# One attention-and-FFN layer in one program: VectorE's first take ahead of the last row half, its inversion behind the second take, and GpSimd's sums beside the exponentials

## What is computed

```python
x = x + xattn(layernorm(x), ctx)       # x: 8 x 1024 x 512, ctx: 8 x 64 x 512, 16 heads of 64
x = x + ffn(layernorm(x))
# xattn: q = ln(x) Wq, k, v = ln(ctx) Wkv; softmax(clip(q k / 8, -11, 11)) v Wo + bo
# ffn:   h = silu(xq Wg) * (xq Wu); out = hq Wd, every operand rounded to 8-bit steps (fake quantization)
```

## Time and profile before

| | us |
|---|---|
| three runs of the kernel, median (lowest, highest) | 1312.22 (1311.52, 1313.82) |
| the profiled execution | 1311.13 |
| its span, first to last instruction | 1309.2 |
| TensorE busy in it | 1263.4 |
| VectorE busy | 1093.7 |
| ScalarE busy | 800.9 |
| GpSimd busy | 277.1 |

### The profile page before, as it was taken

The page is one execution under the profiler, slowest core; times in us unless marked ns, Lnnn a source line. Parts: engine busy times, 40 slices in busy tenths (PEclk is TensorE's granted clock), DMA queues, the critical chain, the costliest instruction groups (busy, mean ns, idle before and its releaser), DMA issues.

```text
span 1309.2 us, 20493 instructions
## 1 busy us (share of the span) xinstructions
PE 1263.4 (96%) x7607; PEld 583.7 (45%) x7607; DVE 1093.7 (84%) x2117; ACT 800.9 (61%) x1211; POOL 277.1 (21%) x227
## 2 busy tenths in 40 slices
PE   6999899999999999999999999999999999999998
PEld 4644444444444444444444443444444444434443
DVE  7777878878877877887787768799999999889998
ACT  6688576567558657756765772233333333399993
POOL 2105231441342144034224330000000000013233
PEclk9999899999999999999999999999999999999999
DMA  8276156248156264452553392196667542389997
GB/s 297 81 234 185 35 144 203 79 108 222 57 140 191 77 179 133 118 197 73 153 197 91 99 245 106 41 307 211 219 257 264 203 170 85 113 313 417 419 418 304
DMA packets 182436, 241.74 MB, mean 185 GB/s; under 512 B 122032, under 2 KB 141248, under 8 KB 169920
## 3 DMA queue, kind: packets, MB, share of 16 engines
q1 hardware_dynamic: 182336, 240.43, 55.8%
HBM read 120.86 MB, written 90.57 MB: 161 GB/s over the span
## 4 chain that ended last, share of the span: by engine, by line
PE 33%; DVE 27%; ACT 16%; POOL 9%; issue 8%; DMA 7%; SPq 1%; POOLq 0%; ACTq 0%; DVEq 0%
PE pg L1575 11%; PE pu L1581 11%; POOL esum L396 8%; ACT hb L1439 4%; ACT E L453 3%; DVE E L668 3%; DVE p L672 3%; ACT E L459 3%; DVE st L608 3%; ACT E L463 2%; PE po L77 2%; PE po L79 2%; PE po L78 2%; DVE st L682 2%; DVE x L679 2%
## 5 line engine op out<-in xcount | busy, mean ns | idle before, releaser
L1417 ACT ACTIVATE sg<-pg,gate_scale 128x512 f32<-128x512 f32 x176 | 120.9, 687 | 183.5 <-PE pg L1575 183.5
L77 PE MATMUL po<-VW,p 128*128 128x512 f16 x480 | 183.4, 382 | 14.0 <-DVE x_rows L679 10.4
L77 PE MATMUL ring<-yT,M 128*128 128x512 f16 x512 | 194.4, 380 | 0.0
L79 PE MATMUL ring<-yT,M 128*128 128x512 f16 x512 | 194.3, 380 | 0.0
L78 PE MATMUL ring<-yT,M 128*128 128x512 f16 x512 | 194.3, 380 | 0.0
L79 PE MATMUL po<-VW,p 128*128 128x512 f16 x480 | 183.2, 382 | 0.0
L78 PE MATMUL po<-VW,p 128*128 128x512 f16 x480 | 183.0, 381 | 0.0
L1575 PE MATMUL pg<-xqT,w 128*128 128x512 bf16 x704 | 180.7, 379 | 1.0 <-ACT xqT L1428 0.8
L1581 PE MATMUL pu<-xqT,w 128*128 128x512 bf16 x704 | 180.7, 380 | 0.0
L474 ACT ACTIVATE p<-E 128x512 f16<-128x512 f32 x120 | 74.7, 623 | 164.1 <-DVE E L668 164.0
L1491 DVE TENSOR_TENSOR hb<-pu,sg 128x512 f32<-128x512 f32 x176 | 120.8, 687 | 26.5 <-PE pu L1581 25.0
(11 more groups left out here) (238 smaller groups left out, 2017.9 us busy)
## 6 DMA issues: line engine op xcount, KB each, us to landing
hidden<-hb SPq DMA_DIRECT2D x11, 2816.0 KB, 9.7
xa<-x_rows_d SPq DMA_DIRECT2D x28, 1024.0 KB, 5.8
hb<-hidden SPq DMA_DIRECT2D x22, 1024.0 KB, 16.2
x<-in_x_dram SPq DMA_DIRECT2D x16, 1024.0 KB, 6.4
value_fold<-E SPq DMA_DIRECT2D x64, 256.0 KB, 2.5
VW<-value_fold SPq DMA_DIRECT2D x16, 1024.0 KB, 6.6
x_rows_d<-x SPq DMA_DIRECT2D x16, 1024.0 KB, 4.1
out_dram<-xa SPq DMA_DIRECT2D x11, 1024.0 KB, 12.9
```

The source lines that it names most:

```text
L77: nc.tensor.matmul(out, a_hi, b_hi, start=first, stop=False)
L79: return nc.tensor.matmul(out, a_lo, b_hi, start=False, stop=last)
L1417: nc.scalar.activation(sg[:, n % 4], pg[n % 4][:], ACT.Silu, scale=gate_scale[:, n % FT:n % FT + 1]).then_inc(silus, 1)
```

## The change

What it does, engine by engine:

- VectorE, steps 2 to 14: the fourth row half of group s+1 (`low_y(s+1, 3)`) moves from the score part behind take 0; `unit_range` moves from in front of take 0 behind folds 0 to 3; `invert` moves from in front of take 1 behind folds 4 to 7. `take` is split in `take_sum` and `take_stats`, which together are the same instructions.
- GpSimd: the adds of a group follow its exponentials in all steps; the four biases come behind the adds, and wait for `prob_lo` only. In step 0 they no longer lie between the adds.
- Steps 0 and 1: statistics and rsqrt of group 2 move from step 0 to step 1; its four rows are normalized and split at the end of step 1. The probabilities of group 0 are divided, made high and low with one tile beside each score tile, where they were bunched later.
- The end (behind the scores of group 15): the inversion comes in front of take 0, the splits of group 15 come earlier among the takes of group 14, the first two takes of group 15 surround `centre`, and `round_unit(14)` goes behind them.

```diff
--- before.py
+++ after.py
@@ -226,17 +226,15 @@
     def highs_beside(s, t):
 
         if s == 1:
-            return ((), (), (0,), (1,), (2, 3), (4,), (5,), (6, 7))[t]
+            return (t,)
         return (t + 2,) if s > 1 and t < 6 else ()
 
     def row_beside(s, t):
 
-        if s + 1 == NG:
-            return None
-        return {5: 2, 7: 3}.get(t) if s == 1 else {3: 0, 4: 1, 6: 2, 7: 3}.get(t)
+        return {3: 0, 4: 1, 6: 2, 7: 3}.get(t) if 1 < s and s + 1 < NG else None
 
     NORM_BESIDE = ((), (), (), (0, 1), (), (2,), (3,), ())
-    LOW_BESIDE = ((), (), (), (), (0,), (1,), (), (2, 3))
+    LOW_BESIDE = ((), (), (), (), (0,), (1,), (), (2,))
 
     FOLD_AFTER = ((0, 1, 2, 3), (4, 5, 6, 7), (), ())
 
@@ -406,14 +404,10 @@
 
         for s in range(NG):
             more = s + 1 < NG
-            if s > 1 and more:
-                pool.wait_ge(prob_lo, 8 * s)
-                pool.wait_ge(y_lo, 4 * (s + 1) + TT)
             for t in range(1, KT):
                 add_up(s, t)
-                if s == 0 and t >= 4:
-                    bias(s + 1, t - 4)
-            if s > 0 and more:
+            if more:
+                wait(pool, prob_lo, 8 * s)
                 for t in range(TT):
                     bias(s + 1, t)
 
@@ -573,9 +567,6 @@
                 if s > 0 and row_beside(s, t) is not None:
                     high_y(s + 1, row_beside(s, t))
                 exp(s, t)
-                if s == 1 and t == 1:
-                    high_y(2, 0)
-                    high_y(2, 1)
                 if s == 0:
                     if t in (0, 2):
                         wo_high(2 + t // 2)
@@ -586,6 +577,9 @@
                         fold_value(0, t)
             if s == 0:
                 continue
+            if s == 1:
+                for t in range(TT):
+                    high_y(2, t)
             for t in range(TT):
                 for u in FOLD_AFTER[t]:
                     fold(s, u)
@@ -671,13 +665,16 @@
             dve.wait_ge(prob_hi, 8 * g + t + 1)
             nc.vector.tensor_tensor(probs(g, 1, t), E[:, g % 2, t], probs(g, 0, t), ALU.subtract).then_inc(prob_lo, 1)
 
-        def take(g, t):
+        def take_sum(g, t):
             if t == 0:
                 dve.wait_ge(x_scaled, g + 1)
             dve.wait_ge(outs, 4 * g + t + 1)
             xt, row = x[:, g % 4, t], keep.rows[:, TT * g + t]
             nc.vector.tensor_tensor_reduce(xt, po[t % 2][:], xt, keep.out_scale[:], -3e38,
                                            ALU.add, ALU.max, row[:, 2:3]).then_inc(outs_taken, 1)
+
+        def take_stats(g, t):
+            xt, row = x[:, g % 4, t], keep.rows[:, TT * g + t]
             dve.wait_ge(outs_taken, 4 * g + t + 1)
             nc.vector.bn_stats(st1[:, t, :], xt).then_inc(x1_step, 1)
             nc.vector.tensor_reduce(row[:, 3:4], xt, AX.X, ALU.min)
@@ -685,6 +682,10 @@
             ins = nc.vector.bn_aggr(row[:, 0:2], st1[:, t, :])
             if t == TT - 1:
                 ins.then_inc(x1_seen, 1)
+
+        def take(g, t):
+            take_sum(g, t)
+            take_stats(g, t)
 
         def unit_range(u):
             dve.wait_ge(f_loaded, 16 * (2 * min(u + 1, FT) + max(u + 1 - FT, 0)))
@@ -928,18 +929,16 @@
                     if t % 2 == 1:
                         fold_value(0, t - 1)
                         fold_value(0, t)
-                    if t == 4:
-                        norm_stats(2)
+                    continue
+                if s == 1:
+                    if t in (2, 3):
+                        norm_stats(2, (2 * t - 4, 2 * t - 3))
                     if t == 5:
                         norm_aggregates(2)
-                    if t == 6:
                         norm_rstd(2, 2)
-                    continue
-                if s == 1:
-                    if t in (4, 6):
-                        norm_rows(s + 1, t // 2)
-                    if t in (5, 7):
-                        low_y(s + 1, t // 2)
+                    if t == 7:
+                        norm_rows(2, 0)
+                        norm_rows(2, 1)
                     continue
                 if not more:
                     continue
@@ -953,47 +952,58 @@
                 for k in NORM_BESIDE[t]:
                     norm_rows(s + 1, k)
             if s == 0:
-                norm_rows(2, 0)
-                norm_rows(2, 1)
                 invert(0)
-                low_y(2, 0)
-                low_y(2, 1)
                 continue
+            if not more:
+                continue
+            if s == 1:
+                for t in range(2):
+                    low_y(2, t)
+                    norm_rows(2, t + 2)
+                low_y(2, 2)
+            take(s - 1, 0)
+            low_y(s + 1, 3)
+            for u in FOLD_AFTER[0]:
+                fold(s, u)
             if s <= UNITS:
                 unit_range(s - 1)
-            take(s - 1, 0)
-            if more:
-                for u in FOLD_AFTER[0]:
-                    fold(s, u)
+            take(s - 1, 1)
+            for u in FOLD_AFTER[1]:
+                fold(s, u)
             invert(s)
-            if more:
-                take(s - 1, 1)
-                for u in FOLD_AFTER[1]:
-                    fold(s, u)
-                round_unit(s - 1)
-                take(s - 1, 2)
-                for u in FOLD_AFTER[2]:
-                    fold(s, u)
-                divide(s, 0)
-                take(s - 1, 3)
-                divide(s, 1)
-                low(s, 0)
+            round_unit(s - 1)
+            take(s - 1, 2)
+            for u in FOLD_AFTER[2]:
+                fold(s, u)
+            divide(s, 0)
+            take(s - 1, 3)
+            divide(s, 1)
+            low(s, 0)
         last = NG - 1
+        unit_range(last - 1)
+        invert(last)
+        take(last - 1, 0)
+        for t in range(3):
+            divide(last, t)
+        low(last, 0)
         take(last - 1, 1)
-        divide(last, 0)
-        divide(last, 1)
-        low(last, 0)
-        round_unit(last - 1)
-        take(last - 1, 2)
-        for t in range(2, KT):
+        low(last, 1)
+        for t in range(3, 5):
             divide(last, t)
             low(last, t - 1)
-            if t == 5:
-                take(last - 1, 3)
+        take_sum(last - 1, 2)
+        for t in range(5, KT):
+            divide(last, t)
+            low(last, t - 1)
         low(last, KT - 1)
+        take_stats(last - 1, 2)
+        take(last - 1, 3)
         keep.range_of_rows(dve, 0, TT * last)
+        take(last, 0)
         keep.centre(dve)
-        for t in range(TT):
+        take(last, 1)
+        round_unit(last - 1)
+        for t in range(2, TT):
             take(last, t)
 
     def on_tensor(pe):
```

## The result

| | before | after |
|---|---|---|
| median of the runs, us (lowest, highest) | 1312.95 (1311.52, 1313.82) | 1292.16 (1290.38, 1292.80) |
| ratio, 95% interval | | 0.9841 [0.9823, 0.9858] |
| the profiled execution, its span | 1311.13, 1309.2 | 1292.56, 1290.8 |

The account below looks back on a forecast made before the run. TensorE, busy 96% of the span, was taken as the bound, so only removing its waits pays. Steady steps -19.5, start +4.8, end -4.3 gave -19.0, written -19.1: 1293 us on the median's scale, range 1287 to 1306.

Parts of the forecast that it names:

- The 12.4 us for the bank: Steady steps: TensorE's twelve waits for VectorE's L679, the sum emptying a PSUM bank, were to go, gaining 12.4 us.
- The 7.1 us of folds: Steady steps: fifteen waits of TensorE's last fold products for VectorE's low halves were to go, gaining 7.1 us.
- The sums beside the exponentials: Steady steps: seven GpSimd adds of 1.27 us per step, each costing VectorE 0 to 1.27 us, were to stay hidden.
- 5 to 7 us a step: Expected sign in steady steps: VectorE's L672, L633 and rsqrt rows up to 1.27 us longer, 5 to 7 us a step.
- The eighth split: Score part: the eighth tile's split was to end at 3.2; TensorE wants it at 4.5, leaving 1.2 us to spare.
- the rivals: One more collision, two more, three or more, change does nothing: 1302.7, 1312.7, 1328, 1313 us; chances 0.13, 0.05, 0.09, 0.03.
- one more add: Rival: another add meets a two-SBUF instruction ahead of the eighth split; 9.6 us lost, 1302.7 us; chance 0.13.
- the cap: Steady steps: the last tile's cap, freeing the ring for the second fold, was to end at 5.8 against 5.9.
- Start: Steps 1 and 2: losses of 10.3 us against 6.2, and 0.7 in step 2: +4.8 us, bounds 0 to +8.
- The half clock: Step 1: a 5.8 us stall at the folds was to halve TensorE's clock again, costing 2.2 us.
- End: Last four outputs: 2.4 us of split waits and 1.9 at low clock were to go: -4.3 us, bounds -2 to -4.3.
- keeps for small waits: In the sum: 0.1 us of the -19.0 us total set aside for small waits, written as -19.1.

## Why the prediction held, point by point

- **The bound** was read rightly: TensorE's waits are the account, and three quarters of the last chain is now TensorE. The 12.4 us for the bank went with the inversion moved behind take 1.
- **The 7.1 us of folds went, but the step that explained them failed.** "Take 0 goes ahead of the last row half ... The 7.1 us go" gave them to that move. Alone it costs 25 us; the inversion alone removes them. I had worked out that VectorE enters the score part over 2 us earlier (first division at 24 instead of 26.6; measured 23.8 to 24.0 and 26.7), and did not ask what that does to the row half a score part later. In the changed kernel it is hidden: there the sums eat that lead (the last cap starts at 4.5 behind the outputs, 4.2 before, 2.5 with the inversion alone), so the move of the row half and of `unit_range` is probably needed again. No run puts them back in the changed kernel. Two ways lead to the same 44.5, and that the fold term came out was in this part luck.
- **The sums beside the exponentials**: mechanism right, sizes off. "5 to 7 us a step" on VectorE was 4.7, because in two of the meetings the add was the longer one instead. The eighth split was to end at 3.2 with 1.2 to spare and ended at 1.8 with 2.7. "By little" was wrong, and so were the rivals' prices: one more add was to cost 9.6 us and cost nothing; six cost 19. That the cap was the other tight place was right, and it binds first, though with more room than told (it ends at 4.9 to 5.5, not 5.8, for 5.9).
- **What the sums' new place buys**: nothing, with VectorE's new order. The prediction called it the added cost and gave it no gain of its own, but did not say that it could be left out.
- **Start**: +3.5 instead of +4.8. The three waits for splits cost 2.9 + 3 x 0.17 = 3.4 us instead of 2.3. The folds came when they were forecast (TensorE goes on 19.6 us behind the outputs, for 19.4), but as TensorE reached them later its wait was 4.2 instead of 5.8. Step 2 lost nothing, for 0.7. The step that put GpSimd's biases in this chain failed: held back they give 0.4 us of wait. The half clock came as told (some 2.5 us for 2.2): 3.4 + 4.2 + 2.5 = 10.1 where 10.3 had been summed.
- **End**: -4.3, as told, though 1.3 of it were clock and not order.
- **Sum**: the total was 0.8 us off. It charged 1.3 us too much to steps 1 and 2, and the other terms are within 0.1; so the attention became 20.2 us shorter for 19.0. What it "keeps for small waits" has the wrong sign (-18.9 was meant, not -19.1), 0.2 us. In the profiled pair the FFN took 1.7 us more, within its scatter, which hides the difference. So being within 1 us is partly luck.

The Trainium skill (SBUF — State Buffer, "Who interferes with whom") says that whoever issues first holds the shared port for its whole instruction and the other blocks. The rows agree in both directions: L69 at 1.14 behind an add, the add at 1.97 behind VectorE's split. It also lists tensor_scalar among the instructions that can take that port; L623, a tensor_scalar with one tensor as input, at 1.50 beside an add agrees.

## What to carry to other kernels

Where an engine has slack, a wait is not local: an instruction that stood too early in one engine's order (here an inversion in front of a take) made another engine late a whole step on, and the second kind of wait looked like a fault of the order around it. Before adding up the gains of several edits from a list of waits, try the edit that stands furthest up the chain alone. One moved line gave here as much as the whole rewrite, and the other half of it alone made the kernel 2% slower.

## What the runs showed of the hardware

Behind waits under 3 us, whether TensorE's clock fell did not follow from their length. Behind waits of 1.86 and 0.38 us it stood at 0.79 over 8 us in the kernel before, and fell to half in the kernel with the row half moved alone too (0.70, then 0.50); behind the same two waits at the same place it stayed at 1.00 in the kernels with the old end, with GpSimd's order alone and with the inversion alone. Behind a wait of 2.84 at a fold it stayed at 1.00. In the kernel with the row half moved alone, thirteen waits of 2.67 to 2.85 us stand at the same place of their steps, and the clock fell behind four of them. In the waits of 4.07 and 3.69 it fell. Behind waits under 3 us the half clock cost 1.2 to 2.2 us where it came; it is thus a chance there and not a term of a sum.
